# Forward transform of the long convolution as two 64-row products of folded time steps, the folding done inside the short-convolution stage

## What is computed

```python
xz = einsum('bld,ed->bel', hidden, W_in)      # 256 -> 2 x 512 channels
x, z = split(xz, 2)
x = silu(causal_conv_4_taps(x) + conv_b)      # along time, per channel
k = s4d_kernel(...)                           # [512, 112], from 8 modes a channel
y = irfft(rfft(x, n=224) * rfft(k, n=224))[..., :112] + x * D
y = einsum('bhl,dh->bld', y * silu(z), W_out)
```

## Time and profile before

| | |
|---|---|
| median of 3 runs | 343.96 us (343.11 to 345.10) |
| the profiled execution | 345.22 us |
| its span in the profile | 343.40 us |
| PE, DVE, ACT, POOL busy, share of the span | 94%, 62%, 44%, 58% |
| convolution stage in steady state | 18.2 to 46.45 us of the span |
| kernel stage and the first transform | 46.45 to 61.4 us |
| steps | to about 191 us, then the expert tiles to 343 us |

### The profile page before, as it was taken

One profiled execution on the slowest core, in us unless ns is written; L12 is line 12 of the kernel. 1 busy time (PEld: TensorE's weight loads), 2 busy tenths in 40 slices (PEclk: granted clock), 3 DMA queues, 4 the chain that ended last, 5 costly groups with the idle time before them and its releaser, 6 DMA issues.

```text
span 343.4 us, 6576 instructions
## 1 busy us (share of the span) xinstructions
PE 323.3 (94%) x1923; PEld 255.1 (74%) x1924; DVE 213.0 (62%) x497; ACT 151.1 (44%) x383; POOL 199.9 (58%) x325
## 2 busy tenths in 40 slices
PE   6999989999899999999999799999999999999970
PEld 2555556566687777787777688899999999999950
DVE  6989996625877789688988246733444533444430
ACT  3688865247255433454343543334422234322320
POOL 4579992324676686766777521513755664556552
PEclk9899999999999999999999899999999999999996
DMA  7920000511566766656466699940110110110120
GB/s 182 364 53 4 0 0 10 186 29 31 168 194 186 194 185 181 205 169 183 110 193 215 209 336 404 320 184 22 68 39 28 32 39 23 31 38 26 35 45 23
DMA packets 19999, 42.43 MB, mean 124 GB/s; under 512 B 3761, under 2 KB 10905, under 8 KB 18554
## 3 DMA queue, kind: packets, MB, share of 16 engines
q1 hardware_dynamic: 17370, 37.32, 33.8%
q0 software_dynamic: 1872, 4.59, 4.9%
q10 hardware_dynamic: 720, 0.08, 0.2%
HBM read 37.16 MB, written 5.34 MB: 124 GB/s over the span
## 4 chain that ended last, share of the span: by engine, by line
PE 78%; DVE 11%; DMA 4%; ACT 2%; POOL 2%; issue 1%; SPq 0%; DVEq 0%; POOLq 0%; ACTq 0%
PE ps L1813 16%; PE ps L1832 14%; DVE stage_b L1128 8%; PE ps L1611 7%; PE ps L1633 7%; PE ps L1500 5%; PE ps L1549 4%; PE ps L1656 4%; PE ps L1550 4%; PE ps L1689 3%; PE ps L1699 3%; PE ps L1660 2%; DMA early<-x_early,early 2%; PE ps L1463 1%; DMA w<-in_x_t 1%; PE ps L1668 1%
## 5 line engine op out<-in xcount | busy, mean ns | idle before, releaser
L1813 PEld LDWEIGHTS ps<-stage_b 128*128 128x128 f32 x480 | 55.8, 192 | 2.3 <-DVE stage_b L1402 0.8
L1813 PE MATMUL ps<-stage_b 128*128 128x128 f32 x480 | 56.2, 276 | 1.2 <-ACT stage_b L1066 1.2
L1832 PE MATMUL ps<-w,stage_b 128*128 x240 | 54.4, 380 | 0.9 <-DVE stage_b L1439 0.9
L1832 PEld LDWEIGHTS ps<-w,stage_b 128*128 128x128 f32 x240 | 44.5, 190 | 6.7 <-issue 1.3
L1280 DVE TENSOR_TENSOR stage_b<-ps,w 112x512 f32<-112x512 f32 x64 | 39.7, 683 | 13.6 <-PE ps L1550 11.5
L720 POOL TENSOR_TENSOR stage_b<-stage_b 112x512 f32<-112x512 f32 x16 | 21.4, 1338 | 37.9 <-DVE stage_b L1280 25.7
L1611 PEld LDWEIGHTS ps<-consts,stage_b 112*128 112x128 f32 x256 | 31.0, 192 | 7.3 <-issue 6.6
L1057 ACT ACTIVATE stage_b<-ps,b 128x128 f32<-128x128 f32 x120 | 32.6, 382 | 5.6 <-issue 5.6
L1066 ACT ACTIVATE stage_b<-ps 128x256 f32<-128x256 f32 x16 | 6.1, 383 | 64.4 <-PE ps L1800 64.4
L790 POOL DMA_INDIRECT stage_b<-x_rows,stage_b x18 | 28.3, 1571 | 7.4 <-issue 5.2
L1128 DVE SCALAR_TENSOR_TENSOR stage_b<-ps,w,stage_b 128x444 f32<-128x444 f32 (+2 forms) x48 | 31.1, 671 | 2.3 <-ACT stage_b L870 1.1
(11 more groups left out here) (217 smaller groups left out, 596.7 us busy)
## 6 DMA issues: line engine op xcount, KB each, us to landing
w<-in_w SPq DMA_DIRECT2D x16, 512.0 KB, 4.6
w<-in_w SPq DMA_DIRECT2D x7, 1024.0 KB, 7.7
w<-in_w SPq DMA_DIRECT2D x16, 256.0 KB, 3.1
stage_b<-in_ctx SPq DMA_DIRECT2D x16, 224.0 KB, 3.2
stage_b<-in_w SPq DMA_DIRECT2D x3, 1024.0 KB, 6.6
w<-in_x_t SPq DMA_DIRECT2D x4, 448.0 KB, 7.0
stage_b<-in_x SPq DMA_DIRECT2D x16, 112.0 KB, 3.6
x_rows<-stage_b SPq DMA_DIRECT2D x16, 112.0 KB, 1.9
```

The lines of the kernel that those rows point to most:

```text
L1813: last_ = m.matmul(ps[:, 2 * par + f // 4, (f % 4) * P:(f % 4 + 1) * P], w1_now[par][:, k, f * P:(f + 1) * P], rows_t[:, par, k * P:(k + 1 ...
L1832: last_ = m.matmul(ps[:, 4 + par, 0:D], h_t[:, par, f * P:(f + 1) * P], w2[:, e, f, :], start=(f == 0), stop=(f == FT - 1))
```

## The change

It uses the symmetry of cosines and sines about the middle of the sequence. Before the transpose, DVE forms the sums and the differences of mirrored time steps (`a_fold`): 57 sums in columns 0 to 56 and 56 differences in columns 64 to 119 of a buffer `folded`. After the transpose the sums lie on partitions 0 to 56 and the differences on 64 to 119, and the forward transform of a sequence is one product over 57 rows and one over 56 rows that starts at partition 64, each still into its own PSUM bank and still 512 columns wide. The even and odd frequency bins share one output of 120 rows. The long kernel's spectrum needs two tables in place of three. Two of the four spectrum products change places, and POOL's addition and subtraction change places.

The convolution stage runs in another order. PE turns a unit five units behind the one it projects, gates 2 to 5 stand behind units 6, 9, 12 and 15, gates 6 and 7 in the tail, gates 8 to 11 in the kernel stage; gates 12 to 15 stay in steps 1 and 2. DVE folds unit u-1 after the taps of unit u. At the start SP issues the chunk of `x_t` before the first block of `w_in` and both before the early constants; ACT loads `ssm` first and issues its three `conv` loads behind its first two exponentials. POOL clears the edges of `conv_x` and `folded`.

```diff
+HF = L // 2
+ODD = 64
+BINS = ODD + HF
...
+    fold = np.zeros((BINS, BINS))
+    fold[:HF + 1] = bins(HF + 1, np.cos, minus_sin)
+    fold[HF] *= 0.5
+    fold[ODD:] = bins(HF, minus_sin, np.cos)
...
-        Z_EARLY, Z_TAIL = 2, 9
+        GATE_BEHIND = (6, 9, 12, 15, 16, 17)
...
@@ sync @@
-            sp.dma_start(consts[:, 0:n_early], ins["consts"][:, 0:n_early]).then_inc(loaded["consts_early"], 16)
...
+            load_hid(0)
             load_w_in(0)
-            load_hid(0)
+            sp.dma_start(consts[:, 0:n_early], ins["consts"][:, 0:n_early]).then_inc(loaded["consts_early"], 16)
...
@@ gpsimd @@
+            g.memset(conv_x[:, :, :, L:L + 1], 0.0)
+            for to in folded:
+                last = g.memset(to[:, :, HF + 1:ODD], 0.0)
+            last.then_inc(edge_set, 1)
...
-                    g.tensor_tensor(y_spec[:, 0, :], prod[:, 0, :], prod[:, 1, :], ALU.subtract)
-                    g.tensor_tensor(y_spec[:, 1, :], prod[:, 2, :], prod[:, 3, :], ALU.add).then_inc(y_set, 1)
+                    g.tensor_tensor(y_spec[:, 0, :], prod[:, 0, :], prod[:, 1, :], ALU.add)
+                    g.tensor_tensor(y_spec[:, 1, :], prod[:, 2, :], prod[:, 3, :], ALU.subtract).then_inc(y_set, 1)
...
@@ scalar @@
-            act.dma_start(log_dt, ins["log_dt"]).then_inc(loaded["ssm"], 16)
             act.dma_start(ssm, ins["ssm"]).then_inc(loaded["ssm"], 16)
-            for dst, name in ((conv_w, "conv_w"), (conv_b, "conv_b"), (d_skip, "d_skip")):
-                act.dma_start(dst, ins[name]).then_inc(loaded["conv"], 16)
+            act.dma_start(log_dt, ins["log_dt"]).then_inc(loaded["ssm"], 16)
...
-                need(act, xt_ps, unit - 1)
+                need(act, fold_set, unit - 1)
...
+                if unit + 2 in GATE_BEHIND:
+                    a_gate(2 + GATE_BEHIND.index(unit + 2))
...
                 a_kernel(h)
-                a_gate(4 + h)
+                a_gate(UNITS // 2 + h)
                 a_spectrum(h)
-            a_gate(8)
...
@@ vector @@
+            def a_fold(unit):
+
+                x_now, to = conv_x[:, unit % 2], folded[unit % 2]
+                dve.wait_ge(act_x, unit + 1)
+                need(dve, xt_ps, unit - 1)
+                v.tensor_tensor(to[:, :, 0:HF + 1], x_now[:, :, 0:HF + 1], x_now[:, :, L:HF - 1:-1], ALU.add)
+                v.tensor_tensor(to[:, :, ODD:], x_now[:, :, 0:HF], x_now[:, :, L:HF:-1], ALU.subtract)\
+                 .then_inc(fold_set, 1)
+
+            dve.wait_ge(edge_set, 1)
             for unit in range(UNITS):
                 a_step(unit // HT, unit % HT)
+                if unit > 0:
+                    a_fold(unit - 1)
+            a_fold(UNITS - 1)
...
@@ tensor @@
                 for h in range(HT):
-                    a_unit(c, h)
-            a_gate(2)
-            a_turn(HT * NC - 2, HT - 2)
-            a_gate(3)
-            a_turn(HT * NC - 1, HT - 1)
-            pe.wait_ge(xt_set, HT * NC)
+                    a_in(c, h)
+                    unit = HT * c + h
+                    if unit >= 5:
+                        a_turn(unit - 5)
+                    if unit in GATE_BEHIND:
+                        a_gate(2 + GATE_BEHIND.index(unit))
+            a_turn(UNITS - 5)
+            a_turn(UNITS - 4)
+            a_gate(6)
+            a_turn(UNITS - 3)
+            a_gate(7)
+            a_turn(UNITS - 2)
+            a_turn(UNITS - 1)
...
-                    m.matmul(ps[0:L, 0, :], const("f_re", L), x_time[:, b, :], start=True, stop=True)
-                    m.matmul(ps[0:L, 1, :], const("f_im", L), x_time[:, b, :], start=True, stop=True)\
+                    pe.wait_ge(xt_set, HT * (b // CB + 1))
+                    m.matmul(ps[0:BINS, 0, :], const("fold")[0:HF + 1], x_time[0:HF + 1, b, :], start=True, stop=True)
+                    m.matmul(ps[0:BINS, 1, :], const("fold")[ODD:BINS], x_time[ODD:BINS, b, :], start=True, stop=True)\
                      .then_inc(dft_ps, 1)
...
-                for s, name in enumerate(("f_re", "f_im0", "f_d")):
+                for s, name in enumerate(("k_re", "k_turn")):
...
             for h in range(HT):
-                a_gate(4 + h)
+                a_gate(UNITS // 2 + h)
                 kernel_spectrum(h)
...
-            a_gate(8)
             pe.wait_ge(spec_set, HT)
             transform(0, 0)
-            a_gate(9)
+            pe.wait_ge(xt_set, UNITS)
             marks_of()
-            a_gate(10)
...
                 if (pair, q) == (0, 1):
-                    a_gate(11)
                     a_gate(12)
```

More of the change, by code:

```diff
@@ L209, in decoder_layer @@
         w_out = r.cut(HT * D).rearrange("p (k d) -> p k d", k=HT)
-        spec = r.cut(3 * H, L).rearrange("p (s h) -> p s h", s=3)
+        spec = r.cut(2 * H, BINS).rearrange("p (s h) -> p s h", s=2)
+        folded = [f.rearrange("p (b t) -> p b t", b=CB) for f in (r.cut(CB * BINS), early[:, 0:CB * BINS])]
         shared = sb("shared", [P, 2048])
@@ L438, in decoder_layer, with turn_bank @@
         UNITS = HT * NC
-        Z_EARLY, Z_TAIL = 2, 9
+        GATE_BEHIND = (6, 9, 12, 15, 16, 17)
+        def turn_bank(unit):
+            return 4 + unit % 2
         def count_bank(n):
@@ L858, in _ @@
             a.activation(km[:, 0, :], ssm[:, 0, :], ACT.Exp).then_inc(k_exp, 1)
+            for dst, name in ((conv_w, "conv_w"), (conv_b, "conv_b"), (d_skip, "d_skip")):
+                act.dma_start(dst, ins[name]).then_inc(loaded["conv"], 16)
             act.wait_ge(k_pool, 2)
@@ L893, in a_unit @@
                     a_step(*((c, h + 1) if h < HT - 1 else (c + 1, 0)))
-                before2 = (c, h - 2) if h >= 2 else (c - 1, h + HT - 2)
-                if not (isinstance(c, int) and before2[0] < 0):
-                    a_move(*before2)
+                if HT * c + h >= 2:
+                    a_move(HT * c + h - 2)
             def a_gate(unit):
@@ L1278, in step @@
                     need(dve, y_set, b)
-                    for n, (x_part, k_part) in enumerate(((0, 0), (1, 1), (0, 1), (1, 2))):
-                        last = v.tensor_tensor(prod[:, n, :], ps[0:L, x_part, :], spec[:, k_part, :], ALU.mult)
+                    for n, (x_part, k_part) in enumerate(((0, 0), (1, 1), (1, 0), (0, 1))):
+                        last = v.tensor_tensor(prod[:, n, :], ps[0:BINS, x_part, :], spec[:, k_part, :], ALU.mult)
                     last.then_inc(prod_set, 1)
@@ L1530, in _ @@
             pe.wait_ge(ends_sb, 1)
-            for n in range(Z_EARLY):
-                a_gate(n)
-            a_turn(0, 0)
-            a_turn(1, 1)
+            a_gate(0)
+            a_gate(1)
             for c in range(1, NC):
@@ L1560, in kernel_spectrum @@
                 need(pe, spec_set, h)
-                for s, name in enumerate(("f_re", "f_im0", "f_d")):
-                    last = m.matmul(ps[0:L, 1 + s, tile], const(name, L), kern_t[:, tile], start=True, stop=True)
+                for s, name in enumerate(("k_re", "k_turn")):
+                    last = m.matmul(ps[0:BINS, 1 + s, tile], const(name, L), kern_t[:, tile], start=True, stop=True)
                 last.then_inc(spec_ps, 1)
@@ L1609, in idft @@
                 for h in range(HT):
-                    for s, name in enumerate(("g_re", "g_im")):
+                    for s, name in enumerate(("g_a", "g_b")):
                         last_ = m.matmul(ps[:, 3, h * L:(h + 1) * L], y_spec[:, s, h * P:(h + 1) * P],
-                                         const(name, L), start=(s == 0), stop=(s == 1))
+                                         const(name, BINS), start=(s == 0), stop=(s == 1))
                 last_.then_inc(idft_ps, 1)
```

95 lines of the change are left out of this document (42 added, 53 removed).

## The result

The changed kernel took 364.01 us in the median of four runs (363.93 to 364.40), the kernel before 343.87 us beside it: 1.058 times as long, with an interval of 1.055 to 1.062. The profiled execution took 364.03 us, its span is 362.1 us against 343.4.

The account below looks back on a forecast made before the run. DVE's taps bound the convolution stage, with PE nearly full, and PE almost all after 49 us. Terms 11.1 + 13 - 0.5 - 2.1 - 1.9 - 1.5 - 1.8 = +16.3 on 343.96 gave 360 us, range 345 to 368.

Parts of the forecast that it names:

- folds themselves: Convolution stage: unhindered fold pairs on DVE, 15 on the path at 0.74 us each, +11.1 us.
- folds standing behind POOL: Convolution stage: folds with two SBUF inputs wait for POOL's running instructions; +13 us, the middle of 10 and 15.
- kernel stage: From last tap to first transform: PE work falls to 2.05 us a block and DVE's reductions become the bound; -2.1 us.
- transforms, all other steps: The 16 transforms: half a product overlaps, 0.43 us, less 0.32 for changes of shape; 0.11 each, -1.8 us.
- the upper case: Convolution stage: waiting POOL takes its turn between a pair's two folds, so the stall is 15 us together.
- only the second half of the first can meet the first half of the second: Transforms: the written order of the halves limits overlap to half a product, 0.43 us.
- The rival built on it: Transforms: whole overlap of the two products, folds still stalled; -8.6 in place of -1.8, 353 us; chance 0.10.
- Without the folds this cover would be gone: Convolution stage: four moved gates, 1.5 us of PE each, are covered at 2.43 us a unit against 2.74.
- The folds do not meet POOL: Convolution stage: L1107 was slow by its broadcast operands, so 13 us fall away; 347 us; chance 0.12.
- the products run one after the other: Transforms: no overlap, only the 0.32 us for changes of shape is left; 367 us; chance 0.10.
- not slower: The 16 transforms pay for the folds, 0.54 us each at whole overlap, if the stall is under 3.5 us; chance 0.10.
- the period: Length of a step as sign of transform overlap: 7.2 us as predicted, 6.8 whole overlap, 7.6 none.

Follow-up runs that it names:

- e8_before_two_tables: The kernel before with two spectrum tables in place of three and the new order at the start, nothing folded; 343.59 us, 1.000 times before.
- e4_before_two_sbuf: The kernel before with two extra, unused DVE additions of 228 elements ahead of each unit's taps, both inputs in SBUF; 367.4 us.
- e9_fold_from_psum: The changed kernel with the SiLU of steps 0 to 56 written to PSUM, so each fold has one input there; 348.26 us, 1.016 times before.
- e1_no_products: The changed kernel with POOL's four large products replaced by memsets, the long kernel's values left out; 344.24 us, of which 6.3 belong to a shorter rest.
- e12_after_filler: The changed kernel with eleven bf16 products on ones in two of PE's gaps at the end of the convolution stage; 362.60 us, 1.054 times before.
- e2_120_rows: The changed kernel with both transform products taken over all 120 rows, zeros in the tables; 368.4 us.
- e11_psum_and_filler: The kernel of e9_fold_from_psum with eleven bf16 products on ones in two of PE's gaps; 348.35 us, 1.011 times before.

## Why the prediction was nearly right, and where its terms were off

The forecast was 360 us, the range 345 to 368, the measured time 364.0. The mechanism that was to decide did: folds with two SBUF inputs stand behind POOL. That the sum came as near as this is in part luck: of the terms below, some were 7.9 us too low together and others 5.6 us too high. Term by term, in microseconds of the two profiled executions:

| term | predicted | measured |
|---|---|---|
| folds themselves | +11.1 | +8.6 |
| folds standing behind POOL | +13 | +15.2 |
| waits for ACT behind a slow PE | none | +1.9 |
| wait for the last SiLU | none | +0.8 |
| start | -0.5 | -0.4 |
| kernel stage | -2.1 | -0.3 |
| from first to second transform | -1.9 | -2.2 |
| step 1, one gate less | -1.5 | -0.4 |
| transforms, all other steps | -1.8 | -4.6 |
| sum | +16.3 | +18.6 (spans: +18.7) |

*The folds.* A pair was put at 0.74 us. It takes 0.61, since two such instructions begin 0.30 us apart; 16 pairs make 9.8, and the table takes off 1.15 us, because a wait for ACT at the start of the stage is gone:

```profile
18.23 4.11 DVE L1128 SCALAR_TENSOR_TENSOR stage_b<-ps,w,stage_b 128x444 f32<-128x444 f32 x6 [1.15 <-ACT stage_b L870]
```

The folds did not do that. In `e8_before_two_tables`, which has none, DVE's taps run without this gap too and the first reduction begins 1.8 us earlier than in the profile of before. From 5 to 18 us the granted clock is 0.87 in the profile of before and 1.00 in those of `e8_before_two_tables` and after. So the 1.15 us belong to the start or to that one execution, which lay 1.3 us above its median, and the folds cost 9.8 us. The prediction also let the SiLU of the last unit run beside the fold before it; but DVE waited 0.77 us for it. The mirrored operand costs nothing: 0.39 and 0.38 us, and a straight pair of 228 elements, beside a quiet POOL, takes 0.39 us each as well (`e4_before_two_sbuf`).

*The turn.* The sum took the middle between 10 and 15 because no row showed who goes next. POOL does: `L1157` shows 4.14 us, a whole product, in both long pairs. With the shorter instructions of POOL at 2.4 us (1.48 + 0.48 + 0.47) the upper case would have been right, 15.2 us.

The Trainium skill, "SBUF — State Buffer", section "SBUF: two separate sides", ties the exclusion to a DVE instruction with two SBUF inputs and a GpSimd instruction that reads SBUF. Both conditions are borne out, each with its opposite: one input in PSUM, 0.39 us (`e9_fold_from_psum`), and POOL's memsets, which read nothing, 0.39 us (`e1_no_products`).

*The transforms.* The step that failed is "only the second half of the first can meet the first half of the second". The two first halves ran together, ahead of the second half of the first product. At whole overlap the prediction had 0.54 us a transform; where PE sets the step it is 7.30 - 6.74 = 0.56. The term was put at -1.8 us and measured -4.6. But over the eleven steps from 115.0 to 191.9 us the mean is 6.99 us against 7.36 before, a gain of 0.37. In the other steps PE waits for what used to be early enough. The chain of waits through such a step:

```profile
120.06 0.56 issue
120.61 1.27 POOL stage_b L736
121.89 1.23 POOL stage_b L737
...
123.17 2.04 PE ps L1633 x16
```

and the group of the inverse transform's weight loads, which before had 7.3 us of idle time ahead of it, 6.6 of that at issue:

```profile
L1633 PEld LDWEIGHTS ps<-consts,stage_b 120*128 120x128 f32 x256 | 29.9, 192 | 11.4 <-POOL stage_b L737 7.5
```

POOL's addition and subtraction are late next. From the fourth to the fifth transform nothing is gained at all (8.14 us in both).

The Trainium skill, "TensorEngine Tiling (Array Packing)", section "Theoretical Speedup", has up to 2x for a contraction of 64 rows or less. The two products take 1.06 us in place of 1.81 in a steady step, 1.7x with the change of shape on the way in, and another 0.20 us falls on the inverse transform behind them (1.97 in place of 1.77 in the chain). The rival built on it was right in its mechanism, for which the prediction had a chance of 0.10; 353 us did not come out because only 4.6 of its 8.6 us reached the time, the stall was larger and PE was slower elsewhere.

*The clock.* This is what the prediction did not have. It costed every PE instruction at the granted clock of 1.00 that the kernel before shows. Its own change made PE idle in three places: behind the standing DVE, between the last turns and the turn of the first block of the long kernel, and in step 0. The lower level that followed cost 1.9 us in waits for ACT, 12.9 - 11.4 = 1.5 us in the kernel stage (the stage takes 11.37 us at a clock of 1.00 in `e12_after_filler` and in `e2_120_rows`) and 8.75 - 7.0 = 1.7 us in step 1, 5.1 us together. That PE alone had room there was seen ("Without the folds this cover would be gone"); that room on PE has a price was not.

*The rivals.* "The folds do not meet POOL" is excluded by the 3.37 and 4.14 us, "the products run one after the other" by the starts 0.01 us apart, and "not slower" needed a stall under 3.5 us. Of the signs named for the changed profile, the chain stayed on DVE until 72 us, the first matmul began at 5.97 us, and the reductions follow one another without gap; the period was on the side named as contrary (6.74), and this part of the prediction was wrong as it said it would be.

What stays open is why step 1 has a mean clock of 0.81 in one kernel and 0.51 in another that does the same in step 0 (`e12_after_filler` and `e11_psum_and_filler`), and whether work for PE in step 0 would keep the clock.

## What to carry to other kernels

Before DVE gets an instruction with both inputs in SBUF, look at what POOL does at that time: each such instruction can stand for a whole instruction of POOL, and two in a row for two; with one input in PSUM it costs only itself. Work saved on an engine is worth only what the chain gives back: here 0.86 us of overlap became 0.56 by the change of shape and 0.37 on average by waits, most of them for POOL, against 0.61 us paid per unit on the engine that bound its stage. And where work is moved off PE, look at its granted clock behind the gaps that this leaves: here the lower level went with about 5 of the 20 us lost.

## What was unexpected of the hardware

- Two float32 products on row groups 0 to 56 and 64 to 119, written one behind the other, run first half beside first half: starts at 135.91 and 135.92, then 136.44 and 136.45. A pass of both takes about 0.53 us where a pass of one product takes 0.43.
- A waiting POOL instruction goes between two DVE instructions with two SBUF inputs that are issued back to back: the second took 4.14 us, twice.
- POOL pays too, but little: its four products took 16.20 us beside the folds and 15.88 beside folds with one input in PSUM.
- Idling and small products on PE in step 0 (2.4 us busy of 4.0, at a granted clock of 0.87 to 1.00) were followed by up to 13.4 us at the lower level, 1.2 GHz (clock 0.51), although PE was busy for all of them.
